# Mixture of experts on 1x1 convolutions: tiles of 448 pixels across images in place of 392 pixels within one

## The reference

```python
x_flat = x.transpose(0, 2, 3, 1).reshape(-1, c)                # x: the normalised images
scores = softmax(x_flat @ gate_w + gate_b, -1)
top_v, top_i = top_k(scores, 2)
top_w = softmax(top_v, -1)
wmap = top_w.T.reshape(2, b, h, w)
present = (top_i[:, :, None] == arange(4)[None, None, :]).any(0)
coef = einsum('ke,kbhw->ebhw', present, wmap)
hdn = relu(einsum('bchw,edc->ebdhw', x, w1) + b1[:, None, :, None, None])
y = einsum('ebdhw,eod->ebohw', hdn, w2) + b2[:, None, :, None, None]
out = einsum('ebohw,ebhw->bohw', y, coef)                       # and the input is added to it
```

## Time and profile before

| | us |
|---|---|
| median of 3 runs | 2576.88 |
| lowest, highest | 2573.12, 2577.55 |
| span of the profiled execution | 2576.7 |
| PE busy in it | 2516.8 (98%) |
| DVE busy | 1743.2 (68%) |
| ACT busy | 999.6 (39%) |
| DMA, mean over the span | 64 GB/s |

### The profile page before, as it was taken

How to read it: one execution, slowest core, us unless ns; L and a number is a source line. 1 busy time by engine, 2 the same in 40 slices (tenths; PEclk the granted TensorE clock), 3 DMA queues, 4 the chain that set the end, 5 groups by cost and what they waited for, 6 DMA issues and landing times.

```text
span 2576.7 us, 40219 instructions
## 1 busy us (share of the span) xinstructions
PE 2516.8 (98%) x14994; PEld 2493.2 (97%) x14994; DVE 1743.2 (68%) x3598; ACT 999.6 (39%) x1833; POOL 74.6 (3%) x44
## 2 busy tenths in 40 slices
PE   5999999999999999999999999999999999999999
PEld 5999999999999999999999999999999999999999
DVE  7776666766666766667666666666667676766663
ACT  3434333434333433343433343434343334443332
POOL 3000000000000000000000000000000000000000
PEclk8999999999999999999999999999999999999999
DMA  4121222112221122212122111222112221112210
GB/s 151 49 68 48 69 77 78 40 48 78 68 78 40 56 69 68 78 49 68 48 68 78 60 57 48 77 69 77 41 49 76 69 77 50 58 57 69 77 59 19
DMA packets 107242, 165.29 MB, mean 64 GB/s; under 512 B 3968, under 2 KB 105600, under 8 KB 107008
## 3 DMA queue, kind: packets, MB, share of 16 engines
q1 hardware_dynamic: 107008, 162.10, 18.7%
HBM read 120.34 MB, written 41.75 MB: 63 GB/s over the span
## 4 chain that ended last, share of the span: by engine, by line
PE 97%; DVE 1%; issue 1%; ACT 0%; DMA 0%; SPq 0%; DVEq 0%
PE z_ps L402 16%; PE y_ps L422 16%; PE y_ps L423 16%; PE y_ps L424 16%; PE z_ps L403 16%; PE z_ps L404 16%; PE g_ps L285 1%; ACT hid L435 0%; DMA b_sb<-in_b 0%; DVE hid L453 0%; DVE xn_rest L257 0%; DVE onehot L365 0%; DVE x_part L266 0%; DVE back L239 0%; DVE x_lo L275 0%
## 5 line engine op out<-in xcount | busy, mean ns | idle before, releaser
L435 ACT ACTIVATE hid<-z_ps,b_sb 128x392 f32<-128x392 f32 x768 | 451.0, 587 | 1076.8 <-PE z_ps L404 1074.5
L453 DVE TENSOR_TENSOR hid<-hid,rows 128x392 f32<-128x392 f32 x768 | 437.9, 570 | 567.6 <-ACT hid L435 558.3
L402 PE MATMUL z_ps<-x_lo,w_hi 128*128 128x392 f32 x2304 | 793.0, 344 | 26.0 <-ACT hid L435 18.0
L422 PE MATMUL y_ps<-h_lo,w_hi 128*128 128x392 f32 x2304 | 785.5, 341 | 2.0 <-DVE h_lo L458 2.0
L403 PE MATMUL z_ps<-x_hi,w_lo 128*128 128x392 f32 x2304 | 785.8, 341 | 0.0
L404 PE MATMUL z_ps<-x_hi,w_hi 128*128 128x392 f32 x2304 | 785.6, 341 | 0.0
L423 PE MATMUL y_ps<-h_hi,w_lo 128*128 128x392 f32 x2304 | 783.6, 340 | 0.0
L424 PE MATMUL y_ps<-h_hi,w_hi 128*128 128x392 f32 x2304 | 782.9, 340 | 0.0
L402 PEld LDWEIGHTS z_ps<-x_lo,w_hi 128*128 128x128 f32 x2304 | 433.7, 188 | 40.3 <-ACT hid L435 22.2
L458 DVE TENSOR_TENSOR h_lo<-hid,h_hi 128x392 fp32r<-128x392 f32 x768 | 430.4, 560 | 11.1 <-issue 11.1
L422 PEld LDWEIGHTS y_ps<-h_lo,w_hi 128*128 128x128 f32 x2304 | 432.4, 188 | 2.5 <-issue 2.3
(11 more groups left out here) (95 smaller groups left out, 785.7 us busy)
## 6 DMA issues: line engine op xcount, KB each, us to landing
rows<-rows_dram SPq DMA_DIRECT2D x63, 1176.0 KB, 6.0
out<-x_raw SPq DMA_DIRECT2D x63, 588.0 KB, 3.5
x_raw<-in_x SPq DMA_DIRECT2D x62, 588.0 KB, 6.9
rows_dram<-wrow SPq DMA_DIRECT2D x32, 98.0 KB
rows<-in_w SPq DMA_DIRECT2D x4, 576.0 KB, 8.4
x_raw<-in_w SPq DMA_DIRECT2D x4, 576.0 KB, 7.2
x_raw<-in_x SPq DMA_DIRECT2D x3, 392.0 KB, 3.8
rows<-rows_dram SPq DMA_DIRECT2D x1, 980.0 KB, 6.4
```

The costliest lines, as they stand in the source:

```text
L402: nc.tensor.matmul(z, w1_hi[:, e, j, ks], lo, start=(j == 0), stop=False)
L422: nc.tensor.matmul(y, w2_hi[:, e, k, ms], h_lo[:, slot], start=first, stop=False)
L435: nc.scalar.activation(hid[:, q % RING], z_ps[:, q % ZB, 0:T], ACT.Relu, bias=b1_sb[:, e, q % NK:q % NK + 1]).then_inc(relu_done, 1)
L453: nc.vector.tensor_tensor(hid[:, q % RING], hid[:, q % RING], rows[:, h, e], ALU.mult).then_inc(scaled, 1)
```

## The change

Four images form a **group** of 3136 pixels, cut into seven tiles of 448. Tiles cross the borders of images, so x_hi and x_lo become rings of two images by pixel, and one tile in seven (`WRAP`, the fourth of a group) has its columns at both ends of the ring: two runs of 224. Each DMA of a tile (rows, residual, store) comes in two pieces, cut at an image border or in the middle.

- The ReLU pass of ACT is gone. `scale` on DVE reads the bank, adds the bias, multiplies by the coefficient and frees the bank; `split_h_hi` and `split_h_lo` take the maximum with zero. Only the first four chunks still have an ACT pass (`relu_early`), which frees their banks. `hid` has three places.
- The residual is fetched a second time, per tile, into `res`; `x_raw` is normalised in place. The bias is one operation per block in place of two (the difference of the ranks' biases by one coefficient row; five rows a tile, not six), and `add_product` adds y and the second bias in three operations.
- The steps of the preparation have new chunk numbers, 21 chunks an image; image 1 is prepared within the first tile's chunks. Its pixels, and the second weights, are fetched earlier. Eight chunks of `mm1` stand ahead of the wait for `present`, not ten. DVE's first scale waits until POOL has done seven of its eight pieces.
- The loop: group 0 is written out, three iterations have two groups (eight images) each, then group 7.

```diff
-T = PIX // HALVES
-UNITS = HALVES * E
+T = 448
+TILES = IMAGES * PIX // T
+UNITS = TILES * E
+TILE_CHUNKS = E * NK
...
+        def moving(tile, j, t):
+            start = T * t % (SLOTS * PIX)
+            if t == WRAP:
+                return tile[:, j].rearrange("p (a b) -> p a b", b=T // 2)[:, 0:TILES:TILES - 1]
+            return tile[:, j, start:start + T]
...
-                    pe.wait_ge(relu_done, CHUNKS * b + NK * u + k - (ZB - 1))
+                elif not (G.first and q < ZB):
+                    pe.wait_ge(scaled, G.chunk(q - ZB + 1))
...
-        def relu(act, b, q):
-            nc.scalar.activation(hid[:, q % RING], z_ps[:, q % ZB, 0:T], ACT.Relu,
-                                 bias=b1_sb[:, e, q % NK:q % NK + 1]).then_inc(relu_done, 1)
-            nc.scalar.copy(h_hi[:, q % RING], hid[:, q % RING]).then_inc(hhi_ready, 1)
-            nc.vector.tensor_tensor(hid[:, q % RING], hid[:, q % RING], rows[:, h, e],
-                                    ALU.mult).then_inc(scaled, 1)
-            nc.vector.tensor_tensor(h_lo[:, q % RING], hid[:, q % RING], h_hi[:, q % RING].bitcast(f32),
-                                    ALU.subtract).then_inc(hlo_ready, 1)
+            dve.wait_ge(z_ready, G.chunk(q + 1))
+            nc.vector.scalar_tensor_tensor(hid[:, q % HIDS], z_ps[:, q % ZB, 0:T], b1_sb[:, e, k:k + 1], coef,
+                                           ALU.add, ALU.mult).then_inc(scaled, 1)
+            nc.scalar.activation(h_hi[:, q % RING], hid[:, q % HIDS], ACT.Relu).then_inc(hhi_ready, 1)
+            nc.vector.scalar_tensor_tensor(h_lo[:, q % RING], hid[:, q % HIDS], 0.0, h_hi[:, q % RING].bitcast(f32),
+                                           ALU.max, ALU.subtract).then_inc(hlo_ready, 1)
...
+        def add_bias(dve, G, t, lk):
+            dve.wait_ge(res_loaded[G.slot(t)], G.uses(t) * 32)
+            for m in range(NJ):
+                xs = res[:, G.slot(t), m]
+                lk.inc(nc.vector.scalar_tensor_tensor(xs, rows[:, G.slot(t), E], bias_gap[:, m:m + 1], xs,
+                                                      ALU.mult, ALU.add))
+        def add_product(dve, G, t, lk):
+            dve.wait_ge(unit_done, G.unit(E * (t + 1)))
+            for m in range(NJ):
+                xs = res[:, G.slot(t), m]
+                nc.vector.scalar_tensor_tensor(xs, y_ps[:, m, 0:T], bias01[:, 1, m:m + 1], xs,
+                                               ALU.add, ALU.add).then_inc(out_ready, 1)
...
-            with eng.Fori(0, (B - 2) // 2) as i:
-                image(i * 2 + 1, 1, False, False)
-                image(i * 2 + 2, 0, False, False)
+            with eng.Fori(0, (GROUPS - 2) // 2) as i:
+                group(Group(i * 2 + 1, 1, i * TILES))
+                group(Group(i * 2 + 2, 0, i * TILES + TILES))
...
+            dve.wait_ge(wlo_ready, 2 * E - 1)
+            scale(dve, Group(0, 0, 0, first=True), 0)
+            def prepare_first(G, q, lk):
+                if q == 0:
+                    stats(dve, main, 1, 1, 0, lk)
+                    stats(dve, main, 1, 1, 1, lk)
+                    group_stats(dve, main, 1, lk)
+                if q == 1:
+                    norm_columns(dve, main, 1, lk)
+                    normalise(dve, main, 1, 1, 0)
+                if q == 2:
+                    normalise(dve, main, 1, 1, 1)
+                    less_part1(dve, main, 1, 1, 0)
+                if q == 3:
+                    split_x_lo(dve, 1, 1, 0)
+                    part3(dve, main, 1, 0)
+                    less_part1(dve, main, 1, 1, 1)
+                if q == 4:
+                    split_x_lo(dve, 1, 1, 1)
+                    part3(dve, main, 1, 1)
```

More of the change, by code:

```diff
@@ L421, in mm2 @@
                     first, last = e == 0 and k == 0, e == E - 1 and k == NK - 1
+                    if first and not (G.first and t == 0):
+                        pe.wait_ge(out_ready, G.tile(t) * NJ - NJ + m + 1)
                     nc.tensor.matmul(y, w2_hi[:, e, k, ms], h_lo[:, slot], start=first, stop=False)
@@ new lines, in store, with load_res @@
+        def store(sp, G, t, out_done, images):
+            sp.wait_ge(out_ready, out_done)
+            for b, (k, lo, n, at) in zip(images, pieces(t % TILES)):
+                sp.dma_start(out_v[b][:, :, lo:lo + n], res[:, G.slot(t), :, at:at + n]).then_inc(stored, 16)
+        def load_res(sp, G, t, images):
+            for b, (k, lo, n, at) in zip(images, pieces(t % TILES)):
+                sp.dma_start(res[:, G.slot(t), :, at:at + n], x_v[b][:, :, lo:lo + n]).then_inc(
+                    res_loaded[G.slot(t)], 16)
@@ new lines, in each_group, with preparing @@
+        def each_group(eng, group):
+            group(Group(0, 0, 0, first=True))
+            with eng.Fori(0, (GROUPS - 2) // 2) as i:
+                group(Group(i * 2 + 1, 1, i * TILES))
+                group(Group(i * 2 + 2, 0, i * TILES + TILES))
+            group(Group(GROUPS - 1, 1, (GROUPS - 2) // 2 * TILES, last=True))
+        def preparing(G, q):
+            for k in range(1, IMAGES + 2):
+                off = q - (PERIOD * k - LEAD)
+                if 0 <= off < PERIOD and not (G.last and k >= IMAGES) and not (G.first and k == 1):
+                    yield k, off
@@ L653, in _ @@
+            each_group(dve, group)
         @block.scalar
@@ L810, in _ @@
-            each_image(sp, image)
+            row = rows_dram[0:1, 0:T].unsqueeze(0).to_broadcast([P, 1, T])
+            sp.dma_start(rows[:, 0, 0:1], row).then_inc(first_row_loaded, 16)
+            for lo, hi in ((1, 3), (3, ROWS)):
+                some = rows_dram[lo:hi, 0:T].unsqueeze(0).to_broadcast([P, hi - lo, T])
+                sp.dma_start(rows[:, 0, lo:hi], some).then_inc(rows_loaded[0], 16)
+            sp.wait_ge(wlo_ready, E + 2)
+            for h in range(HALVES):
+                load_x(sp, main, 1, 1, h)
@@ new lines, in _, with held, next_image @@
+            sp.wait_ge(wlo_ready, 2 * E)
+            load_res(sp, Group(0, 0, 0), 0, [0, 0])
+            sp.wait_ge(main.xlo_ready, HALVES)
+            for h in range(HALVES):
+                load_x(sp, main, 2, 0, h)
+            def held(value):
+                if not isinstance(value, int):
+                    sp.compute_val(value)
+                return value
+            def next_image(b, place_free, k):
+                sp.wait_ge(main.xlo_ready, place_free)
+                for h in range(HALVES):
+                    load_x(sp, main, b, k % SLOTS, h)
@@ L824, in _ @@
             gate_product(pe, main, 0)
-            mm1(pe, 0, 0, 0, first=True)
+            start = Group(0, 0, 0, first=True)
+            mm1(pe, start, 0)
             sum_counts(pe, main)
-            for u in range(1, AHEAD + 1):
-                mm1(pe, 0, 0, u)
-            mm1(pe, 0, 0, AHEAD + 1, chunks=range(1))
+            mm1(pe, start, 1)
+            mm1(pe, start, 2, chunks=range(2))
             pe.wait_ge(flag_ready, 1)
```

565 lines of the change are left out of this document (332 added, 233 removed).

## The result

The changed kernel takes 2565.9 us (median of 4 runs, 2564.4 to 2567.4), the one before 2577.2 on the same chip: ratio 0.9957, 95% interval 0.9945 to 0.9969. It is faster, by 0.43% or 11 us, and inside the range; but the forecast was 2536 us, a gain of 41. Nearly three quarters of the expected gain isn't there, and what came is not made of the parts that were named for it.

A forecast was written before the change was run, and what follows sets the result against it. PE was taken as the bound: start 53.4 + products 2425.2 + gate products 33.2 + turns 4.8 + first-tile stall 15.6 + last add and store 3.4 = 2535.6, called 2536 us; range 2515 to 2567 us, leaving 2 in 10 out.

The forecast's parts named there:

- What bounds the kernel: Whole kernel: PE is busy 98% of the span, so only fewer or shorter PE instructions or fewer gaps save time.
- Wider tiles, 25.9 us: Products on PE: 1728 fewer matmuls at 448 columns, each saving a fixed 15.0 ns, gain 25.9 us.
- 15.0 ns per matmul are not columns: Steady products at 392 columns: 178.4 ns apart, 163.4 of it streaming; the rest taken as fixed cost per instruction.
- the 201.7 of the sum: Forecast time of a 448-column matmul on PE: 448 x 0.4168 + 15.0 = 201.7 ns, used for 12024 products.
- excess per column: Rival for products on PE: the 15.0 ns grow with columns, 203.9 ns a matmul, 2562 us; chance 0.13.
- The floor of 178.4 ns: Rival for products on PE: 178.4 ns is the least spacing, 448 columns need 186.7 to 190, 2355 to 2395; chance 0.07.
- Turns, 28.8 us: Loop turns on PE: 2 left of 14, 2.40 us each, gain 28.8 us; no charge for the longer body.
- DVE, ACT and queues, 0: Steady stretch: DVE takes over freeing the bank, 66% busy against 68%; SP's residual fetch is off the path; cost 0.
- The slower rival: DVE's queue holds PE once per image; 2.8 us on each of 31 images makes 2622 us; chance 0.07.
- Earlier start, 3.0 us: Start: second weights fetched without waiting for POOL, so PE begins second products at 53.4 us, 3.0 earlier.
- Later start, 15.6 us: First tile: image 1's preparation sits in DVE's queue between first chunks, so PE stalls 15.6 us, bounds 8 to 22.

## Why the prediction was wrong

1. **What bounds the kernel**: right. PE is the bound in both, 98%, and the gain lies in the distances between its products: the last one starts 11.3 us earlier, and the span is 11.1 us shorter.
2. **Wider tiles, 25.9 us**: wrong, and the main miss. The step that failed is "15.0 ns per matmul are not columns", carried from one width to another. There is a part that doesn't grow from 256 to 512 columns, but it is 13.3 ns there, 14.1 at 392 and 15.9 or 20.0 at 448. In the kernels it was 178.4 - 163.3 = 15.1 and 204.0 - 186.7 = 17.3. Against the 201.7 of the sum that is 2.3 ns more on each of 12024 products, 28 us: it ate the 25.9 and a little besides, so that the products cost 3.4 us more than before. The rival "excess per column" had the right number (203.9) for the wrong reason; as a rule it is excluded, since 178.4 / 392 a column would make 116.5 at 256 columns and 233.0 at 512, where 120.0 and 226.7 were measured. The floor of 178.4 ns is excluded by the 120.0. The two-run operand cost about 1 ns on 864 products, under 1 us, where the sum took nothing.
3. **Turns, 28.8 us**: the gain is right in size, 33.2, and its reason half right. A turn of before did cost 2.40 us, wherever they were counted, and length cost nothing. But the price isn't of the turn: it is of the place of the loop head. The change happened to have a good one, and that part of its gain is luck; its own head was not moved, but the packet of instructions at its turns and the body with 392 columns say so. I had read the 1.40 us of the earlier trace rows as PE's own, rightly against the releaser that the row names, and did not ask why it came nine products behind the head. The same body with 392 columns paid 5.2 us a turn.
4. **DVE, ACT and queues, 0**: right. No wait of PE past 116 us but at the turns; DVE is busy 63% (66% forecast). The slower rival is excluded.
5. **Earlier start, 3.0 us**: came to 0.5 in the profiled execution. DVE's first scale waited for the rows, not for POOL: the row stands at 52.99 and idle 5.33 us for them, while POOL's seventh piece ended at 51.3. SP wrote image 0's rows out at 46.08 us, at 43.57 before; the sum had taken nothing for rows that come later. In the other runs of the changed body second products began between 53.8 and 55.2, so some of this is scatter.
6. **Later start, 15.6 us**: mechanism and place right, 19.1 measured, within its bounds of 8 to 22. The pixels landed at 57.9, forecast 56.7. What the sum left out is the lower clock behind the long waits, and the waits of 1.2 and 0.7 us for the second tile, a deadline that it took as met.

Steps 2, 3, 5 and 6 explain the total: 28.3 us lost in products, 4.4 more won in turns, 2.4 and 3.5 lost in the start, together 29.8 of the 30.0 us between the sum and the span.

## What to carry to other kernels

A cost per instruction that is read at one width holds at that width; before paying for other widths, run a stream of the products alone at both, which takes one short kernel. When a loop turns, count the instructions between its head and the gap: if the gap stays in its place in the code as the head moves, some instructions ahead of the loop, or fewer turns, remove it, and here that was worth 22 to 30 us without touching the work. Before crediting a large rewrite, try the part of it that is one line.

## What the runs showed of the hardware

- fp32r products of 128 rows by 128 columns of weights stand 13.3 to 15.0 ns above their columns from 256 to 400, 13.3 at 512, and up to 20.0 between; 448 has two levels, 202.6 and 206.7 ns, that each hold for a whole block of 54 products and go with the width of the block before. 512 columns are the cheapest per column of those measured, 0.443 ns.
- A taken loop jump can leave PE without one of its instructions (the 11th, 16th or 19th behind the head) until about 3 us after the jump; up to 6.1 us a turn with the clock's fall. A packet of the instruction queue, 16,384 bytes, lands 1.4 to 2.1 us behind the head, and the late instruction starts 1.2 to 1.6 us after it. With the head moved 24 instructions either way, 0.8 us is left.
- In the kernel with 10 warm-up products, 12 of 14 gaps (2.0 to 2.6 us from start to start) were followed by a stretch at 1.2 GHz, products 327 ns apart in place of 178; in the kernel before (1.5 to 2.0 us), none of 14.
